# Attention-like scores from four column groups: float32 products of raw x in place of split full-width products, spread by transfers

## What is computed

```python
q = (cond @ Wq.T + bq) / sqrt(32)                  # one query per batch
k = x @ Wk.T + bk
v = x @ Wv.T + bv
scores = einsum('bhqd,bhkd->bhqk', q, k)[:, :, 0, :]
attn = clip(scores, 0.0, 1.0)                      # per batch, head, row
context = attn[..., None] * v
out = x + context @ Wo.T + bo
```

## Time and profile before

| what | value |
|---|---|
| median of 3 runs | 184.95 us (184.53 to 186.56) |
| the profiled execution, own time | 185.87 us |
| its span (first to last instruction) | 184.1 us |
| PE / DVE / ACT / POOL busy | 178.1 / 164.5 / 111.7 / 13.4 us |
| granted TensorE clock | 1.00 of full speed throughout |
| HBM read, written | 19.61 MB, 8.39 MB |

### The profile page before, as it was taken

The page is one execution under the profiler, slowest core; times in us unless marked ns, Lnnn a source line. Parts: engine busy times, 40 slices in busy tenths (PEclk is TensorE's granted clock), DMA queues, the critical chain, the costliest instruction groups (busy, mean ns, idle before and its releaser), DMA issues.

```text
span 184.1 us, 2338 instructions
## 1 busy us (share of the span) xinstructions
PE 178.1 (97%) x795; PEld 143.1 (78%) x795; DVE 164.5 (89%) x175; ACT 111.7 (61%) x150; POOL 13.4 (7%) x18
## 2 busy tenths in 40 slices
PE   8999999999899999999999999999999999999990
PEld 2786767888688888888888888888888888878880
DVE  1798469999999997999999999999997999999851
ACT  3568394895776755575587567855466847493200
POOL 6000000000000020211000010121000010111000
PEclk9999999999999999999999999999999999999999
DMA  5999930049220226399788226399720216189786
GB/s 217 347 383 389 395 142 0 12 102 360 103 57 0 57 21 179 49 182 207 215 290 287 58 14 155 91 175 310 227 117 0 57 14 155 62 129 236 201 321 254
DMA packets 9355, 30.24 MB, mean 164 GB/s; under 512 B 1152, under 2 KB 1536, under 8 KB 9216
## 3 DMA queue, kind: packets, MB, share of 16 engines
q1 hardware_dynamic: 7616, 23.81, 35.5%
q0 software_dynamic: 1728, 6.29, 20.6%
HBM read 19.61 MB, written 8.39 MB: 152 GB/s over the span
## 4 chain that ended last, share of the span: by engine, by line
PE 81%; DMA 10%; DVE 3%; SPq 2%; issue 1%; ACT 1%; DVEq 0%
DMA x_raw<-x_t 10%; PE bank_y L350 9%; PE bank_y L352 9%; PE bank_y L354 9%; PE bank_x L350 8%; PE bank_x L354 8%; PE bank_x L352 8%; PE bank_z L354 6%; PE bank_z L352 6%; PE bank_z L350 6%; PE score_bank L412 4%; PE score_bank L413 4%; PE bank_z L467 1%; PE bank_z L466 1%; PE bank_z L465 1%
## 5 line engine op out<-in xcount | busy, mean ns | idle before, releaser
L576 ACT CAST form_hi<-work 128x1024 fp32r<-128x1024 f32 x28 | 29.1, 1051 | 20.8 <-PE score_bank L413 6.6
L832 DVE TENSOR_TENSOR form_lo<-work,form_hi 128x1024 fp32r<-128x1024 f32 (+1 forms) x30 | 35.1, 1185 | 0.9 <-ACT form_hi L576 0.9
L611 ACT ACTIVATE work<-bank_y,const 128x512 f32<-128x512 f32 x30 | 19.8, 686 | 7.9 <-PE bank_y L354 7.6
L817 POOL DMA_DIRECT2D work<-x_t x12 | 10.5, 876 | 153.6 <-DVE work L865 147.8
L350 PE MATMUL bank_x<-form_hi,wo_hi 128*128 128x512 f32 x52 | 20.3, 391 | 0.5 <-issue 0.5
L611 ACT ACTIVATE work<-bank_x,const 128x512 f32<-128x512 f32 x24 | 15.8, 685 | 8.2 <-PE bank_x L354 8.2
L352 PE MATMUL bank_x<-form_lo,wo_hi 128*128 128x512 f32 x52 | 20.2, 389 | 0.0
L354 PE MATMUL bank_x<-form_hi,wo_lo 128*128 128x512 f32 x52 | 20.2, 389 | 0.0
L854 DVE SCALAR_TENSOR_TENSOR work<-relu,work 128x1024 f32<-128x1024 f32 x16 | 19.3, 1220 | 0.3 <-ACT relu L640 0.3
L350 PE MATMUL bank_y<-form_hi,wv_hi 128*128 128x512 f32 x48 | 18.7, 389 | 0.0
L352 PE MATMUL bank_y<-form_lo,wv_hi 128*128 128x512 f32 x48 | 18.7, 389 | 0.0
(11 more groups left out here) (139 smaller groups left out, 375.9 us busy)
## 6 DMA issues: line engine op xcount, KB each, us to landing
x_raw<-x_t SPq DMA_DIRECT2D x16, 512.0 KB, 6.4
out_t<-work SPq DMA_DIRECT2D x14, 512.0 KB, 4.1
work<-x_t POOLq DMA_DIRECT2D x12, 512.0 KB, 5.5
score_others<-score_rows SPq DMA_DIRECT2D x16, 128.0 KB, 2.3
work<-first_t SPq DMA_DIRECT2D x2, 512.0 KB, 3.7
work<-wq_t SPq DMA_DIRECT2D x2, 512.0 KB, 8.8
work<-wk_t SPq DMA_DIRECT2D x2, 512.0 KB, 11.1
work<-wo_t SPq DMA_DIRECT2D x1, 1024.0 KB, 7.4
```

Of the source, the lines that this page charges most:

```text
L576: nc.scalar.copy(flat(form_hi, kind), raw(kind, phase)).then_inc(hi_ready[kind], 1)
L611: nc.scalar.activation(result_set(phase)[:, q, j * ROWS:(j + 1) * ROWS], of[:, j, :], ACT.Identity, bias=bias[:, tile:tile + 1], scale=sca ...
L817: pool.dma_start(output_set(s)[:, q, :], x_t[s, q], accum_op=ALU.add).then_inc(residual_added[q], 16)
L832: return nc.vector.tensor_tensor(to, of, hi.bitcast(F32), ALU.subtract)
```

## The change

- **Scores** are made from raw x, unsplit, by float32 matmuls (`scores(s)`): for each of four k tiles, four matmuls of 32 output columns and 256 rows, one for each group of 32 array columns and partitions, each group with its own quarter of the 1024 rows. Heads now stand on four groups of 32 partitions with 2 copies each (`GROUP` = 32). The weights are one tile, `a_copies`, copied unsplit (`copy_a`); `split_a`, the zeroing and `sum_scores` go.
- **After them** ACT applies relu and bias straight from PSUM, four times 32x256, all into partitions 0 to 31 of `relu` (`clip_scores`), and SP copies these to the other three groups by three transfers of 128 KB (`spread_scores`). Each context product waits for all three.
- **x** has two homes, `x_homes[s % 2]`. The loads of super block 1 are issued at the start without a wait; those of 2 and 3 wait for the score of the super block that had the home before (`next_x`).
- **Order.** PE makes the whole score of a super block in one place; ACT's and DVE's lists are written anew around it. Casts no longer wait for scores.

```diff
-SIDE = P // 2
-COPIES = SIDE // HEADS
-GROUP = BATCH * HEADS
+GROUP = P // 4
+GROUPS = P // GROUP
+COPIES = GROUP // HEADS
+QUARTER = HALF // GROUPS
...
-            def scores(s, half):
...
-                        pe.matmul(bank, a_for_hi[:, b, at + k, :], form_hi[:, kind, k, :], start=first, stop=False)
-                        mm = pe.matmul(bank, a_for_lo[:, b, at + k, :], form_lo[:, kind, k, :], start=False, stop=last)
+            def scores(s):
+                b = s // 2
+                pe.wait_ge(a_ready, b + 1)
+                for q in range(4):
+                    wait(pe, x_loaded[s % 2][q], loads(q, s))
+                if s > 0:
+                    pe.wait_ge(x_t3_ready, s)
+                wait(pe, clipped_ready, GROUPS * (s - 1))
+                for k in range(KT):
+                    for g in range(GROUPS):
+                        half, rows = g // 2, k % 2 * ROWS + g % 2 * QUARTER
...
+                            of = x_raw(s)[:, q, rows:rows + QUARTER]
+                        mm = pe.matmul(score_psum(s)[g * GROUP:(g + 1) * GROUP, :], a_copies[:, b, form, :], of,
+                                       start=k == 0, stop=k == KT - 1)
+                mm.then_inc(score_done, 1)
...
+            def clip_scores(s):
+                act.wait_ge(score_done, s + 1)
...
+                for g in range(GROUPS):
+                    at = slice(g * GROUP, (g + 1) * GROUP)
+                    nc.scalar.activation(relu[0:GROUP, g // 2, g % 2 * QUARTER:(g % 2 + 1) * QUARTER], score_psum(s)[at, :],
+                                         ACT.Relu, bias=c_score[at, b:b + 1]).then_inc(clipped_ready, 1)
...
+            def spread_scores(s):
+                sp.wait_ge(clipped_ready, GROUPS * (s + 1))
+                for g in range(1, GROUPS):
+                    sp.dma_start(relu[g * GROUP:(g + 1) * GROUP, :, :], relu[0:GROUP, :, :]).then_inc(relu_loaded, 16)
...
-                dve.wait_ge(relu_ready, score_number(s, half) + 1)
+                dve.wait_ge(relu_loaded, 16 * (GROUPS - 1) * (s + 1))
...
+            def copy_a(b):
+                dve.wait_ge(a_full_ready, 2)
+                of = a_full[:, :, b * HEADS:(b + 1) * HEADS]
+                nc.vector.tensor_copy(a_copies[:, b, :, :].rearrange("p k (h r) -> p k h r", r=COPIES),
+                                      of.unsqueeze(3).to_broadcast([P, 6, HEADS, COPIES])).then_inc(a_ready, 1)
```

More of the change, by code:

```diff
@@ L233, in load_x, with next_x @@
             def load_x(s, q):
[L234 to L247, removed]
+                sp.dma_start(x_raw(s)[:, q, :], x_t[s, q]).then_inc(x_loaded[s % 2][q], 16)
+            def next_x(s):
+                sp.wait_ge(score_done, s - 1)
+                if s == 2:
                     for n in (0, 2):
@@ L252, in next_x_upper @@
                         sp.wait_ge(wv_lo_ready[form], 1)
[L253 to L267, removed]
+                else:
+                    sp.wait_ge(lo_ready[T4], made(T4, VALUES_AT[s - 2]))
+                for kind, q in ((B11, Q11), (T3, Q12), (B22, Q22), (B21, Q21)):
+                    sp.wait_ge(lo_ready[kind], made(kind, VALUES_AT[s - 2]))
+                    load_x(s, q)
+            def spread_scores(s):
+                sp.wait_ge(clipped_ready, GROUPS * (s + 1))
+                for g in range(1, GROUPS):
+                    sp.dma_start(relu[g * GROUP:(g + 1) * GROUP, :, :], relu[0:GROUP, :, :]).then_inc(relu_loaded, 16)
             def store(s, q):
@@ L521, in _ @@
             product_t2(1)
-            scores(1, 0).then_inc(score_done, 1)
+            scores(1)
             product_t3(1)
@@ L534, in _ @@
                 if what == VALUES:
[L535 to L537 removed]
+                    scores(s)
                 product_t2(phase)
@@ L569, in hi @@
                     act.wait_ge(semaphore, s + 1)
-                before, s_before = PHASES[phase - 1]
-                if before == VALUES and kind in FIRST_PHASE_KINDS and (kind != B22 or s_before == 0):
-                    act.wait_ge(score_done, score_number(s_before, kind in (T3, B22)) + 1)
+                if phase > 1 or kind not in FIRST_PHASE_KINDS:
+                    wait(act, done[kind], 2 * (phase - 1))
+                elif kind == T3:
+                    act.wait_ge(w21_done, 1)
                 else:
-                    wait(act, done[kind], 2 * (phase - 1))
+                    act.wait_ge(first_done, {B11: 2, B21: 4, B22: 8}[kind])
                 nc.scalar.copy(flat(form_hi, kind), raw(kind, phase)).then_inc(hi_ready[kind], 1)
@@ L708, in _ @@
             copy_q_rows()
+            hi(B11, 1)
             hi(T1, 1)
-            first_values(Q12, banks[2], 4)
-            copy_a_rows()
             wo_part(W11, 0)
@@ L1230, in _ @@
             context_t2(7)
+            context(3, Q21)
+            lo(T2, 7)
+            lo(B21, 7)
             context_t3(7)
-            lo(T2, 7)
             context_t4(7)
```

304 lines of the change are left out of this document (122 added, 182 removed).

## The result

The changed kernel takes 179.86 us (median of 6 runs, 179.03 to 179.99), the kernel before 185.94 in the same runs (184.53 to 186.79): a ratio of 0.9668, 95% interval 0.9619 to 0.9718. Forecast were 178.8 us against 184.95, a ratio of 0.967, faster with a chance of 0.90. The forecast holds. Its sum is less right than its total: two terms that it did not have, of opposite sign, cancel by luck.

What follows compares the result with a forecast made beforehand. PE was taken as the bound, with DVE hardly less full. From the profiled 185.87 us, - 6.1 (scores) - 0.5 (gap) + 0.1 (opening) + 0.4 (waits) = 179.8; the median, 0.9 lower, was forecast at 178.8, range 177.0 to 182.4.

Steps and rivals of the forecast that it cites:

- A score at 2.11 us: PE, each super block's score: four k tiles 1.80 us plus 0.31 for the narrow form, against 3.64; 6.1 us saved in all.
- rivals on loads: PE's score bursts: each of eight steps waits 0.108 us for its weight load, a score 2.97 us, 182.2 total; chance 0.12.
- on row count: Rival, PE's score bursts: 256 rows take as long as 512, a score 3.91 us, 186.0 total, no change; chance 0.04.
- on groups in line: Rival, PE's score bursts: column groups run one after another, a score 7.5 us, 200.5 total, slower; chance 0.06.
- the 2.2 at which the prediction had the change lose: PE's score bursts: if fewer than 2.2 of the four column groups overlap, the change loses.
- So PE's own work sets the end: PE, 26 to 171 us, busy 144.27 of 145: each microsecond of matmul removed is won, as long as DVE follows.
- DVE's loss at 6.2 us: DVE: eight sums of halves and part of the weight split go, some 6.2 us, so it does not become the bound.
- the gap of 0.50: PE's wait before 50.56 us for the low part of B11 of phase 2: it goes, 0.5 us saved.
- The opening: PE waits 0.3 us for copy_a_rows, Wo landing at about 23.0; an earlier 0.23 us gap goes, leaving 0.1 net.
- 0.4 us for this and its like: PE waits for T2 of phase 2, its cast on ACT behind score 1's relus: 0.4 us charged, between 0 and 1.
- The spreads: SP's three copies per score: some 4 us behind the last relu, at worst 9; later ones over 5 us of cover.

Runs made afterwards that it cites:

- b2: Changed kernel with the two loops of the score products exchanged, all k tiles of one column group before the next group: ratio 1.0329 to the kernel before.
- c1: Kernel before without the score products with x's low part, 7.3 us less PE work, DVE's sums kept: ratio 0.9883 to the kernel before.
- b4: Changed kernel with eight extra 512-wide DVE passes, two per super block, writing a scratch tile: ratio 0.9912 to the kernel before.
- b1: Changed kernel with every score's sixteen narrow matmuls issued twice in a row: ratio 1.0116 to the kernel before.
- c3: Kernel before with the store of super block 2's last quarter moved behind super block 3's first two stores in SP's queue: ratio 0.9947.

## Why the prediction was right, and where it wasn't

**A score at 2.11 us**: 2.08. Groups side by side, steps that follow the rows, loads that stay hidden: each is in the rows of the burst. Saved are 3.64 - 2.08 = 1.56 us, four times 6.2. The rivals on loads, on row count and on groups in line are out; b2 shows that the last hangs on the order of the loops: in b2 32 steps took the time of 20, an overlap of 1.6, under the 2.2 at which the prediction had the change lose, and b2 did lose, 1.0329.

**"So PE's own work sets the end"**: this step failed as put. c1 took 7.3 us off PE alone and got 2.2. What holds is the condition behind it, "as long as DVE, hardly less full, follows". The prediction priced DVE's loss at 6.2 us (6.3 measured in the page) and gave it no share of the gain. Much of it hung on that: a larger relief of PE without DVE's is worth 2.2 us, and b4, with two thirds of DVE's work put back, loses 4.5 of the 6.1, 2.0 of them in its profile ahead of PE's end and the rest in the tail.

**Waits**: the gap of 0.50 went, with all that belongs to it 0.66 us. The opening was forecast at 0.3 us against the 0.23 that goes; it is 0.60 against 0.39. Wo landed at 23.55 instead of 23.0; in b1 and b2 it landed earlier (22.0 and 23.0) and PE did not wait, so this term varies between executions. "0.4 us for this and its like" was too small: T2 of phase 2 lost 0.77 and B21 of phase 4 0.68. Both come from four relus as one block of 1.95 us in ScalarE's queue (0.49 us each, 0.4 forecast). The second also has a wait that the prediction did not look for: the relus of score 2 wait for DVE's last reader of the tile. Waits sum to +0.21 - 0.66 + 0.77 + 0.68 + 0.40 of chance = +1.4 us where 0.0 was forecast.

**The tail**: no term of the sum. It gave -1.4 us, and c3 takes 1.3 off the tail of the kernel before by moving one store. Whether the change earned it or a residual that happened to land sooner (5.9 us against 8.4) stays open. The sum at PE's end is -6.2 + 1.4 and 0.2 that is left over = -4.6, with the tail -6.0; the forecast had -6.1. The size came out right because the two omissions are equal, which is luck.

**The spreads** took 2.3 us to landing in the median, 2.2 to 3.3 in all; no context product waited for one.

## What to carry to other kernels

Where two engines are both over 95% busy, a saving on one comes through only as far as the other is relieved as well (here 2.2 of 7.3 us alone, 5.1 with both): price both, and test each alone. Follow the time behind the last matmul as its own term: a store that waits for something slow in an in-order queue holds the stores behind it, though their results are ready. Several small operations that replace one on a queue are a block; look for what is wanted right behind them, and let products of different column groups alternate.

## What the runs showed of the hardware

How many column groups overlap hung on the order of their products in the queue: alternating, four at a time, 0.22 us a step for all; group after group, two at a time (b2: 20 steps instead of 8). In b2 records of group 1 start ahead of records of group 0 that were issued before them: "work" at 31.84 ahead of "x_home" at 32.05. The Trainium skill, "TensorE: Matmul & The Clock Gate", Part 3 (Packing small matmuls), has matmuls start strictly in program order; these starts differ, and the measurement decides for this form. A float32 product of 256 rows in 32 columns is two records of one 0.22 us step each. And 32 loads of 109 ns per burst do not show beside the steps, with all rows in use: a step is 0.22 us at 256 rows and 0.45 at 512, with loads of the same length.
